# Both copies of the context mask are loaded into the wide block's idle space during the last self attention, and turned behind the last ranks

## The chip, the cores and the metric

The kernel runs on one core of one Trainium2 chip. The metric is the device time of one execution in microseconds (us), as the median of several runs. The kernel before takes 3855.7 us (three runs, 3854.54 to 3859.91).

An engine's name in a view: PE is TensorE (matmul), PEld its weight load, DVE is VectorE, ACT is ScalarE, POOL is GpSimd, SP is SyncE, whose queue (SPq) starts most of the DMAs. "L1530" is line 1530 of the kernel before.

## The reference

A batch of 4 sequences of 512 tokens (width 256) goes through two layers; each has an attention to a context of 1601 rows and then a block on the tokens alone. Gates (`tanh`) scale what is added to `x`. Cut to its steps:

```python
x = x + tanh(g_xattn[0]) * cross_attention_0(layernorm(x), ctx)        # 16 heads of 64, softmax over 1601
y = layernorm(x)                                                       # gated block 0
y = rmsnorm(y + grouped_query_self_attention(y))                       # 16 heads of 16, 4 of keys and values
y = rmsnorm(y + experts(y))                                            # sigmoid gate, top 2 of 8, capacity 640
x = x + tanh(g_ffn[0]) * y
e = where(mask == 0, -1e20, einsum(q = layernorm(x), k = ctx))         # masked cross attention, 16 heads of 16
x = x + tanh(g_xattn[1]) * (softmax(e / 16) @ ctx @ w_out.T + b_out)   # mask: int32, 512 x 1601
x = x + tanh(g_ffn[1]) * (self_attention(layernorm(x)) + dense_top2_experts(layernorm(x)))
```

The mask is one array for all sequences and heads. The masked attention needs it twice: with queries on the partitions (maskQ, 4 tiles of 128 x 1601) to take the row maxima, and with keys on the partitions (maskT, 12 tiles of 124 x 512 and one of 113 x 512) to add it to the scores.

## The kernel before

The work has four stages: the wide cross attention (block 1) with the self attention of gated block 0 (block 2) woven into it batch by batch; the experts; the masked cross attention (block 3); and block 4 woven into that. The work is a list of units, such as `("turn_e", e, f)`. `build_order` makes the list by a small model of the engines, and every engine then runs through the same list and emits its own part of each unit in that order. So the list is also the order of each queue: SP starts the DMAs of the list one after another, and a DMA whose condition isn't met yet holds up all DMAs behind it.

Most of the memory is two areas per partition, `wide` and `slim`, that the stages use anew. In the wide attention `wide` holds its context, keys, values and exponentials; in the experts stage the same area holds expert weights (`w1_sb`, `w2_sb` from 0), `rows_out` (4096), `rows_in` (6656), `rows_inT` (9216) and `hidden` (11776). `slim` holds block 2's data, and from the experts stage on what block 3 needs: both masks in bf16 (`maskT_sb` at 0, `maskQ_sb` at 3328), keys, values.

At the place of the change (after the last batch of block 2):

- `ranks 3` (DVE) makes the slot numbers of the last batch's tokens; `scatter 3` is 8 indirect DMAs (L1411), whose descriptors POOL makes, that put the token rows into `padded_x` in DRAM.
- `load_rows e` (SP, L961) brings the 640 rows of expert e; experts 0 and 1 first, expert e+2 once `turn_e e` has run on PE. `turn_e` (L1241) transposes them, `up` (L1249) and `down` (L1268) are the two products of an expert. `load_up` (L965) and `load_down` (L968) bring its weights, two experts ahead, `store_rows` (L971) writes its result.
- `mask_keys_in` loads maskT as int32 into `slim` from 6656 on, in two DMAs (L975, L976); DVE turns it into bf16 with -1e20 where the mask is 0 (`mask_keys`, L1530 and L1532). `mask_rows_in` (L978) loads maskQ into the same place and so waits until DVE has turned the first; then DVE turns that (`mask_rows`, L1536).
- Behind these, `load_k` and `load_v` (L981, L985, L986) load context keys and values of the first two groups of block 3, and POOL casts the keys (L1466).

`unit_of_last_down`, `wide_done` (the last PE unit that reads the wide attention's data) and `slim_done` (block 2's last `gate2`) are the marks on which units of later stages wait.

Of the kernel before, what the change touches and what calls it, by code (L numbers as in the profile page):

```python
# [7 lines left out]
B, S, D = 4, 512, 256  # L8
CTX = 1601
# [8 lines left out]
QT = S // P  # L18
FT = D // P
LN_EPS, RMS_EPS = 1e-5, 1e-6  # L20
MASKED = -1e20
# [4 lines left out]
CTX_TILE = 124  # L26
# [9 lines left out]
TOKENS = CAPACITY // P  # L36
HALF = CAPACITY // 2


# [181 lines left out]
def weave(streams, pace, slack):  # L221
# [10 lines left out]
    "setup": (0, 1, 2, 11),  # L232
    "mask_keys": (0, 0, 2, 0), "mask_rows": (0, 0, 1, 0),
    "ln": (0, 1, 14, 0), "turn": (1, 1, 0, 0),
# [26 lines left out]
def landing(unit):  # L261
    k = unit[0]
    if k in ("load_pair", "load_wo", "load_we", "load_up", "load_down", "load_rows", "store_rows"):
        return f"{k}{unit[-1] % 2}", 1
    if k in ("load_k", "load_v"):
        return f"{k}{unit[2] % 2}", {"load_k": 1, "load_v": 2}[k]
    if k in ("load_x", "gather"):
        return f"{k}{unit[1]}", {"load_x": 1, "gather": 2 * QT}[k]
    fixed = {"load_const": 3, "load_small": 10, "load_ctxT": 1, "mask_keys_in": 2, "mask_rows_in": 1, "load_gqa": 3,
             "clear": 3, "scatter": 2 * QT, "load_w4": 2, "store_x": 1}  # L270
    alike = {"mask_keys_in": "mask_in", "mask_rows_in": "mask_in"}
    return (alike.get(k, k), fixed[k]) if k in fixed else None

# [26 lines left out]
def build_order(plan):  # L300
# [21 lines left out]
    def on(unit, *marks):  # L322
        plan.tile_free[unit] = tuple(marks)
        return unit

    def emit(*units):
        order.extend(units)
        return units[-1]
# [199 lines left out]
    def experts_fill(wide_done):  # L528
        hidden_free, xT_free = [wide_done] * 2, [wide_done] * 2
        out_free = [wide_done] * 2  # L530
# [42 lines left out]
    def masks_fill(slim_done):  # L573
        emit(on(("mask_keys_in",), *slim_done))
        yield Step(use=(("ve", 4.0),), name=("mask_keys",), late=15.0)
        unit = emit(("mask_keys",))
        emit(on(("mask_rows_in",), ("vector", unit)))
        yield Step(use=(("ve", 4.0),), needs=(unit,), name=("mask_rows",))
        unit = emit(("mask_rows",))
        for s in range(2):  # L580
            k3_free[s] = v3_free[s] = (("vector", unit),)
        free["b3"] = slim_done
        free["xnT3"] = slim_done
        for g in range(2):
            load_keys(0, g)
        yield Step(use=(("po", 4.0),), needs=(unit,), name=("cast_k", 0, 0), late=6.0)
        emit(on(("cast_k", 0, 0), *free["b3"]))
# [54 lines left out]
    def four_experts(b):  # L642
# [7 lines left out]
        for e in range(EXPERTS):  # L650
# [11 lines left out]
           Stream(each_batch(two_made), 21.9, MADE_2), Stream(each_batch(two_used), 43.4, USED_2)], pace, SLACK_1)  # L662
    emit(*(on((f"load_{n}", e), *wide_done) for e in range(2) for n in ("up", "down")))
    slim_done = (("tensor", ("gate2", B - 1)),)
    emit(*(on(("load_rows", e), *wide_done) for e in range(2)))
    weave([Stream(experts_fill(wide_done), 156.0), Stream(masks_fill(slim_done), 1.0)], pace, SLACK_1)
# [27 lines left out]
def flamingo(nc, t, out):  # L694
    plan = Plan()
    order, bank_of, slot_of = plan.order, plan.bank, plan.slot
    ctx = ExitStack()
    with ctx:
# [110 lines left out]
        maskQ_sb = half(slim, 3328, QT, CTX)  # L809
        mask_keys_i = slim[:, 6656:6656 + NKT * S].bitcast(I32).rearrange("p (k n) -> p k n", k=NKT)  # L810
        mask_rows_i = slim[:, 6656:6656 + QT * CTX].bitcast(I32).rearrange("p (q n) -> p q n", q=QT)
        kq_3 = part(slim, 6656, 2 * (CTX + S))
# [99 lines left out]
        def _(sp):  # L912
            past = Past(sp)
            for unit in order:
# [58 lines left out]
                elif kind == "mask_keys_in":  # L973
                    body, rest_rows = key_rows(t["maskT"])
                    sp.dma_start(mask_keys_i[0:CTX_TILE, 0:full, :], body).then_inc(done_sem, 16)  # L975
                    sp.dma_start(mask_keys_i[0:tail_rows, full, :], rest_rows).then_inc(done_sem, 16)  # L976
                elif kind == "mask_rows_in":
# [23 lines left out]
        def _(pe):  # L1001
            past = Past(pe)
            past.wait_ge(*at("vector", "setup"))
            for unit in order:
# [166 lines left out]
                elif kind == "scoreb":  # L1171
# [7 lines left out]
                    if blk == 3:  # L1179
                        past.wait_ge(*at("vector", "mask_rows"))  # L1180
                        for h in range(2):
                            pe.matmul(head_bank(unit, h), ident_b[0:kn, :], maskT_sb[0:kn, k, :],  # L1182
                                      start=True, stop=False)
# [286 lines left out]
        def _(ve):  # L1470
# [45 lines left out]
            for unit in order:  # L1516
# [11 lines left out]
                elif kind == "mask_keys":  # L1528
                    past.wait_ge(*at("dma", "mask_keys_in"))
                    ve.tensor_scalar(maskT_sb[0:CTX_TILE, 0:full, :], mask_keys_i[0:CTX_TILE, 0:full, :], 0.0, MASKED,  # L1530
                                     ALU.is_equal, ALU.mult).then_inc(vector_done, 1)
                    ve.tensor_scalar(maskT_sb[0:tail_rows, full, :], mask_keys_i[0:tail_rows, full, :], 0.0, MASKED,  # L1532
                                     ALU.is_equal, ALU.mult).then_inc(vector_done, 1)
                elif kind == "mask_rows":
                    past.wait_ge(*at("dma", "mask_rows_in"))
                    ve.tensor_scalar(maskQ_sb, mask_rows_i, 0.0, MASKED, ALU.is_equal, ALU.mult).then_inc(vector_done, 1)  # L1536
                elif kind == "ln":
# [322 lines left out]
```

## Time and profile before

| | |
|---|---|
| median of 3 runs | 3855.7 us (3854.54 to 3859.91) |
| the profiled execution: its own time, its span | 3866.64 us, 3864.7 us |
| PE busy | 3496.2 us (90%), 18248 matmuls |
| DVE busy | 1989.6 us (51%) |
| ACT busy | 1435.3 us (37%) |
| POOL busy | 997.1 us (26%) |
| DMA | 108.28 MB, mean 28 GB/s |
| mean granted clock of TensorE | 0.925 of full speed |
| chain that ended last | PE 84%, DVE 7%, ACT 4%, another core or an unknown queue 2%, POOL 2% |

The time is that of the slowest (here the only) core. The span is what the profile covers of the profiled execution; 1.94 us of its own time lie around it. All times in the rows are us from the start of the span. The profile cuts the span into 40 slices of 96.6 us; PE is busy in nearly all of them at 9 tenths or more, and less in the 20th to the 25th, in which the last self attention, the experts and the start of block 3 lie.

### The profile page before, as it was taken

To read this page: it belongs to the slowest core of one execution; us is meant where nothing else is said; L and a number is where in the kernel's file an instruction comes from. 1 tells how busy PE (TensorE), PEld (TensorE's weight loads), DVE (VectorE), ACT (ScalarE), POOL (GpSimd) and SP (SyncE) were. 2 spreads that over 40 slices of the span, in tenths; PEclk is the share of its full clock that TensorE was granted. 3 is DMA by queue.
4 is the path that set the end of the run, shared out by engine and by line. 5 is a ranking of instruction groups with operands and counts; after the bars stand their busy time and mean duration, and the time that the engine had idled before them with its cause. 6 is when DMAs were issued, how large, how long until landed. Compare 5 with 4: busy or idle time off the path is not lost.

```text
span 3864.7 us, 44052 instructions
## 1 busy us (share of the span) xinstructions
PE 3496.2 (90%) x18248; PEld 1472.8 (38%) x18248; DVE 1989.6 (51%) x3277; ACT 1435.3 (37%) x1639; POOL 997.1 (26%) x481
## 2 busy tenths in 40 slices
PE   7999999989999899998754938989999999999987
PEld 3444443434434344343223812234323422342252
DVE  3445455454654545554330065655665566556444
ACT  3334344333444344443221203342454244334513
POOL 3556445454454554445200030000000000000000
PEclk9999999989999899998767958999999999899987
DMA  3000000000000100000004311010100100010000
GB/s 143 12 12 28 12 12 6 12 34 12 12 6 12 36 10 12 6 8 13 22 12 139 123 57 42 18 35 19 37 20 23 34 23 18 23 34 23 1 17 6
DMA packets 65934, 108.28 MB, mean 28 GB/s; under 512 B 4589, under 2 KB 49285, under 8 KB 65222
## 3 DMA queue, kind: packets, MB, share of 16 engines
q1 hardware_dynamic: 62662, 97.08, 7.9%
q0 software_dynamic: 3072, 8.39, 0.7%
q8 instruction: 143, 2.34, 0.2%
q14 instruction: 57, 0.47, 0.0%
HBM read 88.68 MB, written 16.78 MB: 27 GB/s over the span
## 4 chain that ended last, share of the span: by engine, by line
PE 84%; DVE 7%; ACT 4%; another core or an unknown queue 2%; POOL 2%; issue 1%; DMA 0%; DVEq 0%; ACTq 0%; SPq 0%; POOLq 0%
PE ring L1189 12%; PE pv L1082 10%; PE ring L1071 9%; PE pv L1210 8%; PE ring L1150 4%; PE ring L1052 3%; PE ring L1182 3%; PE ring L1195 3%; PE ring L1068 3%; PE ring L1029 2%; PE ring L1043 2%; PE ring L1044 2%; PE ring L1030 2%; PE ring L1268 2%; PE ring L1097 2%
## 5 line engine op out<-in xcount | busy, mean ns | idle before, releaser
L1452 POOL TENSOR_TENSOR wide<-wide 124x1024 f32<-124x1024 f32 (+1 forms) x352 | 827.9, 2352 | 268.5 <-ACT wide L1351 254.8
L1358 ACT ACTIVATE wide<-ring 124x1024 f32<-124x1024 f32 (+2 forms) x544 | 530.4, 1023 | 641.0 <-PE ring L1189 636.6
L1587 DVE CUSTOM_DVE_ANT_0 slim<-ring,slim 128x802 bf16<-128x802 f32 x512 | 508.3, 993 | 273.0 <-PE ring L1150 239.7
L1351 ACT ACTIVATE wide<-ring 124x1024 f32<-124x1024 f32 (+1 forms) x416 | 425.9, 1025 | 582.7 <-PE ring L1071 547.2
L1571 DVE TENSOR_REDUCE max_a<-ring 128x2 f32<-128x802 f32 x512 | 507.8, 994 | 242.9 <-PE ring L1052 242.4
L1082 PE MATMUL pv<-wide 124*64 124x512 f32 (+1 forms) x1664 | 453.2, 624 | 25.6 <-ACT wide L1351 25.6
L1071 PE MATMUL ring<-wide 64*124 64x512 f32 (+1 forms) x1664 | 429.0, 594 | 0.0
L1189 PE MATMUL ring<-slim 32*128 32x512 f32 x2176 | 405.2, 676 | 11.7 <-DVE slim L1612 7.5
L1597 DVE TENSOR_REDUCE slim<-ring 128x2 f32<-128x1024 f32 x256 | 309.2, 1222 | 192.6 <-PE ring L1162 189.5
L1466 POOL CAST slim<-slim 128x1601 bf16<-128x1601 f32 x16 | 24.4, 1523 | 1315.2 <-DMA slim<-in_ctx_k 965.3
L1150 PE MATMUL ring<-slim 32*128 32x401 bf16 x1024 | 233.2, 360 | 45.8 <-DVE max_b L1587 33.4
L1449 POOL TENSOR_TENSOR wide<-wide 124x1024 f32<-124x1024 f32 x32 | 75.3, 2353 | 637.2 <-PE pv L1082 451.8
L1210 PE MATMUL pv<-wide,slim 124*32 124x512 f32 (+1 forms) x1664 | 223.5, 609 | 1.7 <-ACT wide L1358 1.7
L1189 PEld LDWEIGHTS ring<-slim 32*128 32x128 f32 x2176 | 135.9, 193 | 172.7 <-issue 100.0
L1082 PEld LDWEIGHTS pv<-wide 124*64 124x64 f32 (+1 forms) x1664 | 83.5, 136 | 265.4 <-issue 214.4
L1052 PE MATMUL ring<-wide 64*128 64x401 bf16 x1024 | 175.8, 340 | 7.1 <-DVE max_a L1571 5.8
L1068 PE MATMUL ring<-wide,select_b 64*128 64x512 bf16 x832 | 160.8, 383 | 14.2 <-ACT wide L1351 12.2
L1150 PEld LDWEIGHTS ring<-slim 32*128 32x128 bf16 x1024 | 56.1, 95 | 293.6 <-ACT wide L1358 132.8
L1071 PEld LDWEIGHTS ring<-wide 64*124 64x124 f32 (+1 forms) x1664 | 157.3, 185 | 22.5 <-issue 2.9
L1561 DVE CAST wide<-wide 128x800 bf16<-128x800 f32 x64 | 37.1, 579 | 244.4 <-ACT wide L1328 174.7
L1043 PE MATMUL ring<-wide 128*124 128x128 f32 (+1 forms) x832 | 160.0, 274 | 0.0
L1044 PE MATMUL ring<-wide 128*124 128x128 f32 (+1 forms) x832 | 159.4, 272 | 0.0
(233 smaller groups left out, 4084.0 us busy)
## 6 DMA issues: line engine op xcount, KB each, us to landing
slim<-in_ctx_k SPq DMA_DIRECT2D x16, 800.5 KB, 4.4
wide<-in_w_pair SPq DMA_DIRECT2D x32, 384.0 KB, 3.1
slim<-in_ctx_v SPq DMA_DIRECT2D x16, 744.0 KB
wide<-in_w SPq DMA_DIRECT2D x16, 512.0 KB, 5.2
wide<-in_we SPq DMA_DIRECT2D x16, 512.0 KB, 3.6
wide<-in_ctxT SPq DMA_DIRECT2D x4, 1601.0 KB, 7.4
wide<-padded_x SPq DMA_DIRECT2D x8, 640.0 KB, 7.3
expert_rows<-wide SPq DMA_DIRECT2D x8, 640.0 KB, 3.8
```

What stands on the lines that cost most here:

```text
L1052: last = pe.matmul(slot[:, h * BANK:h * BANK + CHUNK], queries_ab[own, q * P:(q + 1) * P], keys_ab[own, c0:c0 + CHUNK], start=True, stop=True)
L1071: last = pe.matmul(slot[0:kn, h * BANK:(h + 1) * BANK], keys_a[own, p % 2, k0:k0 + kn], queries_a[own, p % 2, :], start=False, stop=True)
L1082: last = pe.matmul(pv_a[64 * h:64 * h + 64, :], values_a[0:kn, p % 2, k, 64 * h:64 * h + 64], exps_a[0:kn, slot_of["scorea", b, p, k], h * ...
L1150: last = pe.matmul(slot[:, j * BANK:j * BANK + CHUNK], queries_low(3, g)[own, q * P:(q + 1) * P], keys_low(3)[own, c0:c0 + CHUNK], start=T ...
L1189: last = pe.matmul(head_bank(unit, h), key_columns(blk, g, k0)[own, :], queries_place(blk, g)[own, :], start=blk != 3 or h >= 2, stop=blk ...
L1210: last = pe.matmul(pv_of[blk][PAD * h:PAD * h + PAD, :], value_columns(blk, g, k, kn, h), exps_tile(blk, b, g, k, h)[0:kn, :], start=k == ...
L1351: sc.activation(exps_a[0:kn, slot_of[unit], :], slot[0:kn, :], ACT.Exp, scale=WIDE ** -0.5).then_inc(scalar_done, 1)
L1358: sc.activation((exps_2 if blk == 2 else exps_34)[0:kn, first + 2 * i:first + 2 * i + 2, :].rearrange("p h n -> p (h n)"), ring_t[0:kn, ba ...
L1452: po.tensor_tensor(sums[0:kn, :], sums[0:kn, :], view, ALU.add).then_inc(pool_done, 1)
L1571: ve.reduce_max(max_a[:, :, q, c], slot.rearrange("p (h n) -> p h n", h=2)[:, :, 0:CHUNK], AX.X).then_inc(vector_done, 1)
L1587: ve.tensor_tensor_reduce(out=max_junk.rearrange("p (j n) -> p j n", j=2), in0=two[:, :, 0:CHUNK], in1=maskQ_sb[:, q, c0:c0 + 2 * CHUNK].r ...
L1597: ve.tensor_reduce(neg_cols[blk][:, q, 2 * hp * PAD:2 * hp * PAD + PAD + 1:PAD], slot.rearrange("p (h n) -> p h n", h=2), AX.X, ALU.max, n ...
```

## The change

The list is changed around the experts' start, and with it where the int32 masks lie.

- The int32 masks no longer go to `slim` but into parts of `wide` that the wide attention has left: maskQ where `rows_inT` and `hidden` come to lie (from 9216), nine tiles of maskT from 15872, the other four (three full, one of 113 rows) where `rows_out` comes to lie (from 4096). The two no longer share a place.
- Both loads are emitted behind the first experts' weights and wait for `wide_done` alone. maskT is loaded in three DMAs instead of two.
- DVE turns both right behind `ranks 3` and waits for `slim_done`, since the bf16 masks overwrite block 2's data; it does so in four instructions instead of three, and each mask has its own semaphore.
- The first evacuations of `turn_e` wait for `mask_rows`, those of `up` for `mask_keys` (ACT).
- `load_k`, `load_v` and `cast_k` of the first groups wait for `slim_done` only, but are emitted later in the list: behind `turn_e 3`, before the second half of `down 1`, where they stood behind `turn_e 2` before.

```diff
 COUNTS = {
-    "mask_keys": (0, 0, 2, 0), "mask_rows": (0, 0, 1, 0),
+    "mask_keys": (0, 0, 3, 0), "mask_rows": (0, 0, 1, 0),
...
     def experts_fill(wide_done):
-        hidden_free, xT_free = [wide_done] * 2, [wide_done] * 2
+        hidden_free, xT_free = [(("vector", ("mask_keys",)),)] * 2, [(("vector", ("mask_rows",)),)] * 2
...
     def masks_fill(slim_done):
-        emit(on(("mask_keys_in",), *slim_done))
-        yield Step(use=(("ve", 4.0),), name=("mask_keys",), late=15.0)
-        unit = emit(("mask_keys",))
-        emit(on(("mask_rows_in",), ("vector", unit)))
-        yield Step(use=(("ve", 4.0),), needs=(unit,), name=("mask_rows",))
-        unit = emit(("mask_rows",))
+        yield Step(needs=(("turn_e", 3, 1),))
         for s in range(2):
-            k3_free[s] = v3_free[s] = (("vector", unit),)
+            k3_free[s] = v3_free[s] = slim_done
...
-        yield Step(use=(("po", 4.0),), needs=(unit,), name=("cast_k", 0, 0), late=6.0)
+        yield Step(use=(("po", 4.0),), name=("cast_k", 0, 0), late=6.0)
...
     emit(*(on((f"load_{n}", e), *wide_done) for e in range(2) for n in ("up", "down")))
+    emit(on(("mask_rows_in",), *wide_done), on(("mask_keys_in",), *wide_done))
     slim_done = (("tensor", ("gate2", B - 1)),)
+    emit(on(("mask_rows",), *slim_done), on(("mask_keys",), *slim_done))
     emit(*(on(("load_rows", e), *wide_done) for e in range(2)))
...
-        mask_keys_i = slim[:, 6656:6656 + NKT * S].bitcast(I32).rearrange("p (k n) -> p k n", k=NKT)
-        mask_rows_i = slim[:, 6656:6656 + QT * CTX].bitcast(I32).rearrange("p (q n) -> p q n", q=QT)
+        mask_keys_i = wide[:, 15872:15872 + STAGED * S].bitcast(I32).rearrange("p (k n) -> p k n", k=STAGED)
+        mask_rest_i = wide[:, 4096:4096 + (NKT - STAGED) * S].bitcast(I32).rearrange("p (k n) -> p k n", k=NKT - STAGED)
+        mask_rows_i = wide[:, 9216:9216 + QT * CTX].bitcast(I32).rearrange("p (q n) -> p q n", q=QT)
...
-                    sp.dma_start(mask_keys_i[0:CTX_TILE, 0:full, :], body).then_inc(done_sem, 16)
-                    sp.dma_start(mask_keys_i[0:tail_rows, full, :], rest_rows).then_inc(done_sem, 16)
+                    sp.dma_start(mask_keys_i[0:CTX_TILE, :, :], body[:, 0:STAGED, :]).then_inc(done_sem, 16)
+                    sp.dma_start(mask_rest_i[0:CTX_TILE, 0:full - STAGED, :], body[:, STAGED:full, :]).then_inc(done_sem, 16)
+                    sp.dma_start(mask_rest_i[0:tail_rows, full - STAGED, :], rest_rows).then_inc(done_sem, 16)
```

In SP's queue, from the first experts' weights (`w1`, `w2` of experts 0 and 1) to the second stored result, `in_maskT` and `in_maskQ` are the masks, `padded_x` the experts' rows, `in_ctx_k` and `in_ctx_v` keys and values of block 3. Before:

```order
84 L965 DMA wide<-in_w1 128x1024
85 L968 DMA wide<-in_w2 128x1024
86 L961 DMA wide<-padded_x 128x5x256 x2
87 L975 DMA slim<-in_maskT 124x12x512
88 L976 DMA slim<-in_maskT 113x512
89 L978 DMA slim<-in_maskQ 128x4x1601
90 L961 DMA wide<-padded_x 128x5x256 x2
91 L965 DMA wide<-in_w1 128x1024 x2
92 L961 DMA wide<-padded_x 128x5x256
93 L981 DMA slim<-in_ctx_k 128x1601
94 L985 DMA slim<-in_ctx_v 124x12x128
95 L986 DMA slim<-in_ctx_v 113x128
```

And the same stretch now (the lines of the new kernel are one to two lower here):

```order
85 L966 DMA wide<-in_w2 128x1024
86 L977 DMA wide<-in_maskQ 128x4x1601
87 L973 DMA wide<-in_maskT 124x9x512
88 L974 DMA wide<-in_maskT 124x3x512
89 L975 DMA wide<-in_maskT 113x512
90 L959 DMA wide<-padded_x 128x5x256 x4
91 L963 DMA wide<-in_w1 128x1024 x2
92 L959 DMA wide<-padded_x 128x5x256
93 L969 DMA expert_rows<-wide 128x5x256
94 L966 DMA wide<-in_w2 128x1024
95 L963 DMA wide<-in_w1 128x1024
96 L959 DMA wide<-padded_x 128x5x256
```

The masks stand ahead of the first two experts' rows, the rows of experts 2 and 3 directly behind those, and the keys and values (from row 97 on) one expert later.

On DVE, at the end of `ranks 3` (the last two small operations) and the start of the experts' results. Before:

```order
798 L1800 TENSOR_TENSOR prob<-combine,pick 128x32
799 L1802 TENSOR_REDUCE shares<-prob 128x4 [waits vector_done]
800 L1530 TENSOR_SCALAR slim<-slim 124x6144 [waits landed_mask_in]
801 L1532 TENSOR_SCALAR slim<-slim 113x512
802 L1536 TENSOR_SCALAR slim<-slim 128x6404 [waits landed_mask_in]
803 L1809 COPY wide<-ring 128x768 [waits tensor_done]
```

Now:

```order
799 L1807 TENSOR_REDUCE shares<-prob 128x4 [waits vector_done]
800 L1541 TENSOR_SCALAR slim<-wide 128x6404 [waits landed_mask_rows_in]
801 L1531 TENSOR_SCALAR slim<-wide 124x4608 [waits landed_mask_keys_in]
802 L1533 TENSOR_SCALAR slim<-wide 124x1536
803 L1535 TENSOR_SCALAR slim<-wide 113x512
804 L1814 COPY wide<-ring 128x768 [waits tensor_done]
```

The turns keep their place in DVE's order, but the rows' mask now comes first and the keys' mask takes three instructions. They wait for loads that stand further ahead in SP's queue, past the ones for the experts' rows.

## Rows read from the trace of the kernel before

**Rows 1.** Page, the span in 40 slices: granted clock of TensorE in tenths

```profile
PEclk9999999989999899998767958999999999899987
```

**Rows 2.** Windows: stretch, busy by engine (instructions), clock, DMA share, GB/s

```profile
2054.40:2100.80 46.40, 0.00 (x0) 0.00 (x0) 5.63 (x3) 0.70 (x1) 0.00 (x0) 0.54 0.40 132
2100.80:2113.00 12.20, 12.17 (x51) 10.78 (x52) 2.51 (x2) 1.41 (x2) 1.52 (x1) 0.80 0.75 258
2113.00:2230.00 117.00, 117.00 (x520) 94.25 (x519) 11.55 (x14) 24.12 (x35) 0.00 (x0) 1.00 0.38 120
```

**Rows 3.** Timeline of PE: start, us, line, operation, tile, count, [idle before <-releaser]

```profile
2036.50 17.89 PE L1249 MATMUL ring<-wide 128*128 128x320 f32 x64
2100.83 2.37 PE L1241 MATMUL ring<-consts,wide 128*128 128x128 f32 x10 [46.45 <-DMA wide<-padded_x]
2102.99 10.12 PE L1268 MATMUL ring<-wide 128*128 128x256 f32 x40
...
2121.57 1.25 PE L1241 MATMUL ring<-consts,wide 128*128 128x128 f32 x10
2122.66 8.80 PE L1268 MATMUL ring<-wide 128*128 128x256 f32 x40
...
2141.13 8.87 PE L1268 MATMUL ring<-wide 128*128 128x256 f32 x40
...
2177.89 8.80 PE L1268 MATMUL ring<-wide 128*128 128x256 f32 x40
```

**Rows 4.** Timeline of SP's queue, DMA issues from 1867 to 2135 us

```profile
1867.48 0.43 SPq L968 DMA_DIRECT2D wide<-in_w  x1
2027.60 0.95 SPq L961 DMA_DIRECT2D wide<-padded_x  x2
2028.59 0.47 SPq L975 DMA_DIRECT2D slim<-in_maskT  x1
...
2088.47 0.40 SPq L978 DMA_DIRECT2D slim<-in_maskQ  x1
2088.91 1.07 SPq L961 DMA_DIRECT2D wide<-padded_x  x2
...
2103.23 0.38 SPq L961 DMA_DIRECT2D wide<-padded_x  x1
...
2134.91 1.26 SPq L968 DMA_DIRECT2D wide<-in_w  x1
```

**Rows 5.** Timeline of DVE, the turns of the masks

```profile
2084.74 3.36 DVE L1530 TENSOR_SCALAR slim<-slim 124x6144 bf16<-124x6144 int32 x1 [68.78 <-DMA slim<-in_maskT]
2088.02 0.42 DVE L1532 TENSOR_SCALAR slim<-slim 113x512 bf16<-113x512 int32 x1
...
2098.86 3.50 DVE L1536 TENSOR_SCALAR slim<-slim 128x6404 bf16<-128x6404 int32 x1 [10.42 <-DMA slim<-in_maskQ]
```

**Rows 6.** Timeline of POOL, first and last of the last scatter's eight

```profile
2016.25 0.98 POOL L1411 DMA_INDIRECT padded_x<-src,places  x1 [158.58 <-DVE shares L1802]
...
2025.17 0.97 POOL L1411 DMA_INDIRECT padded_x<-src,places  x1 [0.30 <-issue]
```

**Rows 7.** Timeline around 825 us, a POOL addition and DVE beside it

```profile
822.38 4.86 POOL L1452 TENSOR_TENSOR wide<-wide 124x1024 f32<-124x1024 f32 x2 [0.18 <-ACT wide L1351]
...
825.33 1.95 DVE L1780 TENSOR_TENSOR prob<-prob,hit 128x32 f32<-128x32 f32 x1
...
827.42 0.19 DVE L1785 TENSOR_TENSOR prob<-prob,pick 128x32 f32<-128x32 f32 x1
```

**Rows 8.** Timeline around 2247 us, indirect DMAs of POOL and DVE beside them

```profile
2247.09 0.95 POOL L1421 DMA_INDIRECT wide<-expert_rows,sources  x1 [0.30 <-issue]
2248.34 1.07 POOL L1421 DMA_INDIRECT wide<-expert_rows,sources  x1 [0.30 <-issue]
...
2247.32 3.38 DVE L1729 SCALAR_TENSOR_TENSOR src<-wide,shares,src 128x256 f32<-128x256 f32 x8 [15.69 <-DMA wide<-expert_rows,sources]
```

**Rows 9.** Windows: the stretch from block 3 in full swing to the end

```profile
2440.00:3865.00 1425.00, 1336.12 (x7109) 501.18 (x7108) 808.70 (x1519) 559.83 (x610) 20.76 (x14) 0.93 0.08 22
```

More of the change, by code:

```diff
@@ L37 @@
 HALF = CAPACITY // 2
+STAGED = 9
 HOP = 0.2
@@ L268, in landing @@
         return f"{k}{unit[1]}", {"load_x": 1, "gather": 2 * QT}[k]
-    fixed = {"load_const": 3, "load_small": 10, "load_ctxT": 1, "mask_keys_in": 2, "mask_rows_in": 1, "load_gqa": 3,
+    fixed = {"load_const": 3, "load_small": 10, "load_ctxT": 1, "mask_keys_in": 3, "mask_rows_in": 1, "load_gqa": 3,
              "clear": 3, "scatter": 2 * QT, "load_w4": 2, "store_x": 1}
-    alike = {"mask_keys_in": "mask_in", "mask_rows_in": "mask_in"}
-    return (alike.get(k, k), fixed[k]) if k in fixed else None
+    return (k, fixed[k]) if k in fixed else None
 class Plan:
@@ L1179, in _ @@
                     if blk == 3:
-                        past.wait_ge(*at("vector", "mask_rows"))
+                        past.wait_ge(*at("vector", "mask_keys"))
                         for h in range(2):
@@ L1529, in _ @@
                     past.wait_ge(*at("dma", "mask_keys_in"))
-                    ve.tensor_scalar(maskT_sb[0:CTX_TILE, 0:full, :], mask_keys_i[0:CTX_TILE, 0:full, :], 0.0, MASKED,
+                    for lane, other in plan.tile_free[unit]:
+                        past.wait_ge(*at(lane, *other))
+                    ve.tensor_scalar(maskT_sb[0:CTX_TILE, 0:STAGED, :], mask_keys_i[0:CTX_TILE, :, :], 0.0, MASKED,
                                      ALU.is_equal, ALU.mult).then_inc(vector_done, 1)
-                    ve.tensor_scalar(maskT_sb[0:tail_rows, full, :], mask_keys_i[0:tail_rows, full, :], 0.0, MASKED,
+                    ve.tensor_scalar(maskT_sb[0:CTX_TILE, STAGED:full, :], mask_rest_i[0:CTX_TILE, 0:full - STAGED, :], 0.0, MASKED,
+                                     ALU.is_equal, ALU.mult).then_inc(vector_done, 1)
+                    ve.tensor_scalar(maskT_sb[0:tail_rows, full, :], mask_rest_i[0:tail_rows, full - STAGED, :], 0.0, MASKED,
                                      ALU.is_equal, ALU.mult).then_inc(vector_done, 1)
@@ L1535, in _ @@
                     past.wait_ge(*at("dma", "mask_rows_in"))
+                    for lane, other in plan.tile_free[unit]:
+                        past.wait_ge(*at(lane, *other))
                     ve.tensor_scalar(maskQ_sb, mask_rows_i, 0.0, MASKED, ALU.is_equal, ALU.mult).then_inc(vector_done, 1)
```

## The prediction

> **What bounds the kernel now.** I read the page's chain first: PE has 84% of it, so an edit counts only where PE stands still or waits to restart. The slices say where: the granted clock of TensorE falls to 5 to 7 tenths in the middle and is 9 almost everywhere else [rows 1]. The windows there are clear-cut. From 2054.4 to 2100.8 us PE does nothing at all, the clock is 0.54 and the DMA engines are busy 40%; the next 12.2 us run at 0.80, and then 117 us at 1.00 with PE busy all of the time [rows 2]. So one hole of 46.4 us lies in the experts stage, and behind it PE is the bound.
>
> The timeline of PE names the hole's end: the transposes of expert 2 waited 46.45 us for its rows (`padded_x`) [rows 3]. SP's queue tells why they were late. The rows of experts 0 and 1 went out at 2027.60, maskT at 2028.59, and then SP stood at maskQ until 2088.47, because maskQ was to go where the int32 maskT still lay; the rows of experts 2 and 3 stood behind it and went out at 2088.91 [rows 4]. DVE could turn maskT only at 2084.74, after 68.78 us of idling for it [rows 5]. The load of maskT takes 2084.74 - 2028.59 = 56.15 us; maskQ, slightly larger, took 2098.86 - 2088.47 = 10.4 us [rows 4, 5]. The chain is thus: scatter, slow maskT load, turn, SP released, rows land, PE. The idle time is no lack of bandwidth, but the order of a queue.
>
> **The change part by part.**
>
> *The hole.* SP no longer waits for DVE. The rows of experts 2 and 3 go out when PE has transposed those of experts 0 and 1, before the 64 `up` matmuls that begin at 2036.50 and end at 2054.39 [rows 3]. A pair of such loads took from 2088.91 until the wait ended at 2100.83, 11.9 us [rows 3, 4]; begun at 2036.5 they land by 2048.4, 6 us before PE wants them. So all of the 46.45 us goes.
>
> *The restart.* After the hole PE ran at a low clock (0.80 over 12.2 us [rows 2]). Ten transposes took 2.37 us where the next expert's took 1.25, and forty `down` matmuls 10.12 where the next took 8.80 [rows 3]: 1.12 + 1.32 = 2.44 us. Without the hole PE goes from one matmul to the next, so this goes too. Together **-48.9 us**.
>
> *The loads of the masks.* They now follow the first experts' weights, at about 1868 [rows 4], and need 10.4 + 56.15 = 66.6 us one behind the other, if the three DMAs of maskT move as the two did. They land by about 1935, 81 us before the last ranks end at 2016 (POOL starts on them at 2016.25 [rows 6]). Block 2 takes all its data from on chip in that time and SP issues nothing between 1868 and 2027 [rows 4], so nothing is behind them: 0 us. If that cover were gone, each us beyond 2016 would show in the first evacuations of the experts, on ACT.
>
> *The turns.* DVE works 3.50 + 3.36 + 0.42 = 7.28 us as before, some 0.1 more for the fourth instruction. It starts at 2016.0, where it idled [rows 5], and is done at 2023.3; behind it in DVE's queue are only the first experts' results. The evacuations that now wait for it come after the rows have landed, later than 2032. On DVE that is 0. But POOL makes the descriptors of the last scatter from 2016.25 to 2026.14, eight times [rows 6], and the whole chain to PE waits for that scatter. In the trace before, DVE idles through all of it. What does 7.3 us of DVE work beside it cost? The lower end is almost nothing: beside eight DVE operations of 0.42 us each, one of POOL's indirect DMAs took 1.07 us against 0.95 [rows 8]. The upper end is that they exclude each other: a tiny DVE operation took 1.95 us instead of 0.19 while POOL's addition ran, and ended with it at 827.28 [rows 7]. Then the first indirect DMA starts at 2023.3 instead of 2016.25: 7.0 us. I take **+7.0**. The turns are single instructions of up to 3.5 us, back to back, reading and writing SBUF only; they leave no gaps as the short ones of [rows 8] do, and the one place where the trace shows the two engines in each other's way shows a wait to the other's very end.
>
> The Trainium skill has a rule for exactly this ("SBUF — State Buffer", "Who interferes with whom"): a DVE cast or tensor_scalar in a two-port mode and GpSimd hold the same port pair as an exclusive lock, and whoever comes second stands still; the section before it adds that GpSimd then cannot write descriptors. By that rule the cost is the 7.0; it also says that operations with two SBUF inputs probably don't hold up descriptors, and with that the 0.12 us of [rows 8] agrees. No row here has such a DVE operation beside a scatter.
>
> *Keys and values.* SP issues the four large loads of block 3's keys and values right behind an expert's rows. Before, that was behind the rows of expert 4; from their issue at 2103.23 to that of the next weights for `down` (expert 2) at 2134.91 SP needed 31.7 us, mostly on them [rows 4]. `down 2` began at 2141.13, 37.9 us after 2103.23, and 18.47 after `down 1` (2122.66), where two experts together take 2177.89 - 2141.13 = 36.76, or 18.38 each [rows 3]. So the weights were just in time, at the most 0.1 us late. Now the loads go out one expert later, behind the rows of expert 5, and `down 3` must have its weights. From those rows' issue to `down 3` are two experts less the 0.2 us between `down`'s start and the issue, 36.5 us. The margin shrinks by 1.4 us, since the slow restart is no longer in it. The cost lies between 0 (the queue is emptier than at 2103) and 1.5; I take **+1.0**. The result of expert 1 is stored later, but its place is written again only by `down 3`'s evacuation.
>
> *Sum.* -48.9 + 7.0 + 1.0 = -40.9 us. In the profiled execution: 3866.64 - 40.9 = 3825.7. The median of the runs was 3855.7, 10.9 lower than this execution, so the forecast for the median is 3855.7 - 40.9 = **3814.8 us**, 1.1% less.
>
> **The rivals.**
>
> *The scatter is not held up.* For it: rows 8, 0.12 us. Then the turns are free, the sum is -47.9, and the time 3807.8. Against it: these are long instructions without gaps.
>
> *The keys and values starve `down 3` and what follows.* SP needs 31.7 us for them whatever PE does, and the margin is spent. If the weights of `down 3` and then those of `up 5` each come some 5 us late (the loads wait behind the values' small packets), the sum is -48.9 + 7 + 10 = -31.9, 3823.8. Against it: before, the second set behind the block was no problem, since PE ran without a gap from 2113 to 2230 [rows 2].
>
> *The change doesn't do what it says.* If the masks landed after the ranks, ACT would hold the experts instead. maskT would have to take over 81 us longer than its 56. Each us beyond that costs one; at 20 us late the time is 3834.8. Against it: nothing else uses the DMA engines there.
>
> *Slower: the hole was a rest that paid for clock.* From 2440 on PE is busy 1336.12 of 1425 us at a mean clock of 0.93 [rows 9]. If PE without its pause were granted less there, its busy time would grow. Since 40.9 us are gained, the time is that of before when 1336.12 x (0.93 / c - 1) = 40.9, at a mean clock of c = 0.902; at 0.89 it costs 60.1 us, and the time is 3874.9. Against it: PE has run 117 us without a gap at 1.00 [rows 2], and the low clocks there stand in and behind its idle time.
>
> **How the numbers follow.** The forecast has 0.58 (delayed scatter, small loss on the weights), the free scatter 0.27, starved weights 0.09, late masks 0.03, the slower case 0.03. The medians of two sets of runs differ by about 3 us by chance (the three of before span 5.4). For 8 times in 10 the range takes the free scatter with that error, 3807.8 - 3.3, and goes up to the starved case: 3804.5 to 3823.5. A change of this kernel's time is told from none at about 0.2%, 7.7 us. All cases but the slower one and half of the late masks are far beyond that: faster 0.95, same 0.02, slower 0.03.
>
> **What would show it.** In the new profile the window behind the first 64 `up` matmuls has PE busy throughout, and the transposes of expert 2 take 1.25 us. DVE's turns lie at 2016 to 2023.3 and do not wait for a DMA. The first of POOL's last eight scatters shows right or wrong the 7.0: it lasts some 8 us, or starts late, or is 1 us as before, and PE's first expert transposes begin at 2039 instead of 2032.17. At `down 3` PE waits 0 to 1.5 us for `in_w`. The forecast is wrong if PE waits for the masks through ACT, if a new gap of more than a few us stands at `down 3` or `up 5`, or if the mean clock from the experts on falls below 0.93.

## The result and the profile after

| | before | after |
|---|---|---|
| median | 3855.1 us (4 runs, 3846.6 to 3859.9) | 3816.6 us (4 runs, 3813.3 to 3820.2) |
| profiled execution: own time, span | 3866.64, 3864.7 us | 3817.63, 3815.6 us |
| mean granted clock | 0.925 | 0.932 |

The ratio is 0.9893 with a 95% interval of 0.9868 to 0.9918: 1.1% faster, 32 to 51 us. 3814.8 us was forecast.

The windows around the experts, in the order of the columns of [rows 2]:

```profile
2035.60:2057.40 21.80, 21.79 (x86) 16.18 (x87) 0.00 (x0) 9.03 (x12) 0.00 (x0) 0.91 0.30 100
2057.40:2112.00 54.60, 54.60 (x246) 43.88 (x245) 4.95 (x6) 12.02 (x18) 1.52 (x1) 1.00 0.49 149
2112.00:2185.00 73.00, 72.92 (x328) 59.37 (x326) 7.56 (x9) 14.01 (x20) 0.00 (x0) 1.00 0.34 112
```

PE is busy from the first transposes to the last `down`, and the clock goes up to 1.00 and stays there. Nothing is left of the hole of [rows 2]. PE's timeline answers [rows 3] (L1240 is the transposes, L1248 `up`, L1267 `down`; before they were L1241, L1249, L1268):

```profile
2035.58 4.30 PE L1240 MATMUL ring<-consts,wide 128*128 128x128 f32 x20 [25.66 <-DMA wide<-padded_x]
2039.88 17.49 PE L1248 MATMUL ring<-wide 128*128 128x320 f32 x64
2057.21 1.26 PE L1240 MATMUL ring<-consts,wide 128*128 128x128 f32 x10
2058.30 8.80 PE L1267 MATMUL ring<-wide 128*128 128x256 f32 x40
...
2112.23 1.25 PE L1240 MATMUL ring<-consts,wide 128*128 128x128 f32 x10
2113.57 8.87 PE L1267 MATMUL ring<-wide 128*128 128x256 f32 x40
...
2167.57 17.43 PE L1267 MATMUL ring<-wide 128*128 128x256 f32 x80
```

The transposes of expert 2 follow the first `up` with no wait and take 1.26 us instead of 2.37, the first `down` 8.80 instead of 10.12. At `down 3` (2113.57) there are 1.34 us from the transposes' start instead of the usual 1.09. In SP's queue (as [rows 4]; L977 maskQ, L973 to L975 maskT, L959 the experts' rows, L966 weights for `down`) the masks went out at 1866.6 and the rows of four experts in one go:

```profile
1866.61 0.46 SPq L977 DMA_DIRECT2D wide<-in_maskQ  x1
1867.11 0.46 SPq L973 DMA_DIRECT2D wide<-in_maskT  x1
1867.61 31.15 SPq L974 DMA_DIRECT2D wide<-in_maskT  x1
1898.80 11.44 SPq L975 DMA_DIRECT2D wide<-in_maskT  x1
2031.03 9.23 SPq L959 DMA_DIRECT2D wide<-padded_x  x4
...
2107.42 1.32 SPq L966 DMA_DIRECT2D wide<-in_w  x1
```

And DVE and POOL at the end of the ranks, both engines of one timeline in order of time (answers to [rows 5] and [rows 6]):

```profile
2014.16 0.19 DVE L1807 TENSOR_REDUCE shares<-prob 128x4 f32<-128x32 f32 x1
2014.27 3.49 DVE L1541 TENSOR_SCALAR slim<-wide 128x6404 bf16<-128x6404 int32 x1
2014.63 5.71 POOL L1410 DMA_INDIRECT padded_x<-src,places  x1 [158.31 <-DVE shares L1807]
2017.67 2.55 DVE L1531 TENSOR_SCALAR slim<-wide 124x4608 bf16<-124x4608 int32 x1
2020.13 0.96 DVE L1533 TENSOR_SCALAR slim<-wide 124x1536 bf16<-124x1536 int32 x1
2020.64 1.29 POOL L1410 DMA_INDIRECT padded_x<-src,places  x1 [0.30 <-issue]
2021.02 0.41 DVE L1535 TENSOR_SCALAR slim<-wide 113x512 bf16<-113x512 int32 x1
2022.23 0.97 POOL L1410 DMA_INDIRECT padded_x<-src,places  x1 [0.30 <-issue]
...
2028.61 0.97 POOL L1410 DMA_INDIRECT padded_x<-src,places  x1 [0.30 <-issue]
```

DVE no longer waits for a DMA. But the first indirect DMA of the scatter takes 5.71 us where it took 0.98, the second 1.29; from the third on they are as before. The eight start over 13.98 us instead of 8.92: the scatter is 5.06 us late.

**Where the time went.** One stretch can be compared without the luck of the clock elsewhere: from the end of the ranks (end of DVE's last small reduction) to the end of the last `down`. Before: 2015.97 to 2230.90, 214.93 us. After: 2014.35 to 2185.00, 170.65 us. The difference of -44.28 us has four pieces. From the ranks' end to the first transposes: 16.20 before, 21.23 after, +5.03. To the end of the first 64 `up` matmuls: 22.22 and 21.79, -0.43. From there to `down 0`: 48.60 and 0.93, -47.67. The rest: 127.91 and 126.70, -1.21, namely the slow restart of `down` gone (-1.32), `down 3` later (+0.31), and a delay of `down 2` gone. The spans differ by 49.1; the other 4.8 us lie ahead of the stretch (1.6) and behind it (3.2), where the work is unchanged. The medians differ by 38.5. The stretch differed by 1.4 us between two executions of the changed kernel (170.65 and 172.01, below); a median of this kernel is known to several us.

### The profile page after: what moved, and what is told of

It reads as the page before. It is cut to its first block and busy times, and to the rows that moved or that the text cites. A ratio compares the mean times of both kernels' runs of the same rounds, so it can differ in the third digit from the quotient of the medians.

```text
span 3815.6 us, 44056 instructions
## 1 busy us (share of the span) xinstructions
PE 3487.2 (91%) x18248; PEld 1464.8 (38%) x18248; DVE 1989.9 (52%) x3278; ACT 1435.6 (38%) x1639; POOL 1002.5 (26%) x481
## 5 line engine op out<-in xcount | busy, mean ns | idle before, releaser
L1592 DVE CUSTOM_DVE_ANT_0 slim<-ring,slim 128x802 bf16<-128x802 f32 x512 | 508.6, 993 | 273.7 <-PE ring L1149 240.9
L1188 PE MATMUL ring<-slim 32*128 32x512 f32 x2176 | 403.9, 674 | 11.7 <-DVE slim L1617 7.5
L1067 PE MATMUL ring<-wide,select_b 64*128 64x512 bf16 x832 | 160.8, 383 | 14.2 <-ACT wide L1350 12.2
```

The costliest lines, as they stand in the source:

```text
L1188: last = pe.matmul(head_bank(unit, h), key_columns(blk, g, k0)[own, :], queries_place(blk, g)[own, :], start=blk != 3 or h >= 2, stop=blk ...
L1592: ve.tensor_tensor_reduce(out=max_junk.rearrange("p (j n) -> p j n", j=2), in0=two[:, :, 0:CHUNK], in1=maskQ_sb[:, q, c0:c0 + 2 * CHUNK].r ...
```

## The experiments

The kernels ran on three chips, each beside executions of before on the same chip: the change once more, the turns behind the scatter (alone and with the values split) and the split of maskT beside 11 of before (median 3864.9 us); the last two rows beside 7 (3861.0); the three marked "once" ran once each beside one of before (3848.3), so their ratio has no interval. The stretch is the one above. "Wait" is PE's wait with a releaser between the first `up` and the last `down`.

| kernel | first indirect DMA | ranks' end to first transposes | PE's wait | stretch | ratio to before (95%) |
|---|---|---|---|---|---|
| before | 0.98 | 16.20 | 46.45 | 214.93 | 1 |
| after | 5.71 | 21.23 | none listed | 170.65 | 0.9893 (0.9868 to 0.9918) |
| the change once more | 5.71 | 21.23 | 1.44 | 172.01 | 0.9904 (0.9885 to 0.9922) |
| turns behind the scatter | 0.98 | 16.13 | 2.31 | 170.05 | 0.9856 (0.9833 to 0.9879) |
| the same, a reduction beside it | 0.99 | 16.15 | 1.59 | 167.74 | 0.9873, once |
| one turn beside it | 3.98 | 19.13 | 2.85 | 173.65 | 0.9927, once |
| short turns beside it | 1.13 | 16.71 | 2.49 | 168.91 | 0.9881, once |
| before, maskT split | 0.99 | 16.17 | 11.08 | 178.59 | 0.9910 (0.9892 to 0.9929) |
| turns behind, values split | 0.98 | 16.20 | none | 165.92 | 0.9856 (0.9832 to 0.9879) |
| that once more | 0.98 | 16.17 | none | 165.74 | 0.9889 (0.9868 to 0.9909) |
| another order, masks in slim, loads split | 0.99 | 16.16 | none | 165.72 | 0.9865 (0.9845 to 0.9884) |

### The change once more

> The changed kernel once more, unedited, beside the others on the same chip. Expected 1.0 to 1.2% below the kernel before, near 3815 us; the first of the last eight indirect DMAs takes 5.7 us again, the PE stretch from the first expert transposes to the end of the last down takes 149.4 us.

Measured: 3827.9 us beside a before of 3864.9, 1.0% less (before on this chip was 10 us slower than beside the first runs, so the 3815 us expected were not met, but the ratio was). The 5.71 us are as expected. From the first transposes to the last `down`'s end it took 2176.81 - 2026.03 = 150.8 us instead of 149.4; the 1.4 us more are a wait at `down 3` (below).

### What holds up the scatter: the turns moved

```diff
 elif kind == "mask_rows":
     past.wait_ge(*at("dma", "mask_rows_in"))
+    past.wait_ge(*at("dma", "scatter", B - 1))
```

> The changed kernel, with one more wait: DVE turns the masks only when the last scatter has landed. My theory (DVE's turns shut POOL out while it makes the scatter's descriptors): the first of POOL's last eight indirect DMAs takes 0.98 us instead of the 5.71 of the changed kernel, PE's first expert transposes start 16.2 us after the ranks end instead of 21.2, and the turns (7.4 us) lie beside the load of the experts' rows and the first up matmuls, where at most the first evacuation waits for the rows' turn (0 to 2 us). Time 3 to 5 us below the changed kernel, about 3812. Rival (the scatter was slow for another reason: more DMA traffic, or descriptor memory): the first indirect DMA still takes over 5 us and the time is that of the changed kernel, or 2 us more from the later turns.

The first indirect DMA is back at 0.98 us and the first transposes start 16.13 us behind the ranks: the turns had held it up. The theory's 3 to 5 us did not all reach the stretch (170.05 against 170.65 and 172.01). The first transposes and `up` took 22.44 us instead of 21.79, and `down 3` gave most of the rest back:

```profile
2096.41 1.26 PE L1240 MATMUL ring<-consts,wide 128*128 128x128 f32 x10
2099.97 10.49 PE L1267 MATMUL ring<-wide 128*128 128x256 f32 x40 [2.31 <-DMA wide<-in_w]
```

A wait of 2.31 us and a slow restart of 1.69 (10.49 against 8.80). The median, 3808.7, is 19 us below that of the change once more on the same chip, far more than the 2 us of the stretch. The two profiled executions differ by 2.0 us (3811.7 and 3809.7), both at a mean granted clock of 0.936; the other four of the change took 3826 to 3832 us at 0.930 or 0.931. So the rest goes with the clock, and nothing ties it to this edit: two sets of runs of one kernel (values split, and that once more) differ by 0.0033 in their ratio, some 13 us. That this edit frees the scatter is shown by the timeline, not by the time.

### Is it DVE being busy, or the kind of its operation?

Against the kernel with the turns behind the scatter:

```diff
     past.wait_ge(*at("dma", "mask_rows_in"))
+    ve.reduce_max(max_b[:, 0, 0, 0:1], wide[:, 9216:9216 + 6404], AX.X).then_inc(vector_done, 1)
     past.wait_ge(*at("dma", "scatter", B - 1))
```

> The kernel that turns the masks after the last scatter, with one extra DVE operation beside the scatter: a maximum over 6404 values per partition in SBUF (about 6.7 us), whose result nobody uses. Theory (what shuts POOL out is the kind of the turns, which move two values per cycle, not DVE being busy): the first indirect DMA takes about 1 us although DVE is busy as long as with the turns. Rival (any long DVE operation on SBUF holds POOL up, or DVE's bandwidth does): it takes 5 us or more.

DVE and POOL in the timeline:

```profile
2005.92 6.81 DVE L1539 TENSOR_REDUCE max_b<-wide 128x1 f32<-128x6404 f32 x1
2006.29 0.99 POOL L1410 DMA_INDIRECT padded_x<-src,places  x1 [149.68 <-DVE shares L1809]
2007.58 0.97 POOL L1410 DMA_INDIRECT padded_x<-src,places  x1 [0.30 <-issue]
```

DVE reads SBUF for 6.81 us in one instruction, and POOL takes 0.99 us where it took 0.98. So it is not DVE being busy that holds POOL up, but the kind of operation. The reduction takes 6.81 us for 6404 values, the turn 3.49 for as many: the turn moves values about twice as fast. The section that the prediction quoted from the Trainium skill ("SBUF — State Buffer", "Who interferes with whom") names `tensor_scalar` in a two-port mode as an operation that shuts GpSimd out and `tensor_reduce` as one that on this chip never does. The trace agrees with both (5.71 and 0.99 us).

The reduction also writes one value per partition where the turn writes 6404, and this run doesn't separate that from the rate. Rows of the changed kernel at the start of block 3 speak against the writing: from 2221.57 to 2230.02 POOL's indirect DMAs took 0.94 to 0.95 us each beside DVE operations (L1592) that write 802 values per partition to SBUF in 0.99 us. A slow writing operation as long as a turn was not run.

### How long POOL waits

One turn alone beside the scatter:

```diff
 elif kind == "mask_keys":
     past.wait_ge(*at("dma", "mask_keys_in"))
+    past.wait_ge(*at("dma", "scatter", B - 1))
```

> The changed kernel, but only the rows' mask (3.5 us, one instruction) is turned beside the last scatter; the keys' mask waits until the scatter has landed. Theory A (POOL waits for the DVE instruction that runs, and would have gone between the first two if it had been asked to): the first indirect DMA takes 0.98 + 3.1 = about 4.1 us at the most, and the scatter ends 2.5 to 3.5 us late instead of 5.06. Theory B (POOL was only held from the second turn on): the scatter is 1 us late or less.

```profile
2006.20 3.49 DVE L1542 TENSOR_SCALAR slim<-wide 128x6404 bf16<-128x6404 int32 x1
2006.57 3.98 POOL L1410 DMA_INDIRECT padded_x<-src,places  x1 [149.67 <-DVE shares L1808]
2010.85 0.97 POOL L1410 DMA_INDIRECT padded_x<-src,places  x1 [0.30 <-issue]
```

Theory A: 3.98 us, 3.00 late. POOL's instruction ends at 2010.55, 0.86 us behind the turn's end at 2009.69, which is nearly its whole undisturbed length. With all four turns (the changed kernel) it ends at 2020.34, only 0.12 behind the end of the second turn (2020.22). Both would fit if POOL needed what DVE holds twice, early in the instruction and again at its end: it got the first at the boundary between the turns (2017.7), worked, and was shut out again by the second turn until 2020.2. The traces show the ends; the two accesses are a guess from them that no run tested.

The same turns in 29 short instructions:

```diff
-    ve.tensor_scalar(maskQ_sb, mask_rows_i, 0.0, MASKED, ALU.is_equal, ALU.mult)
+    for q in range(QT):
+        for c0, c1 in ((0, 400), (400, 800), (800, 1200), (1200, CTX)):
+            ve.tensor_scalar(maskQ_sb[:, q, c0:c1], mask_rows_i[:, q, c0:c1], 0.0, MASKED, ALU.is_equal, ALU.mult)
...
-    ve.tensor_scalar(maskT_sb[0:CTX_TILE, 0:STAGED, :], mask_keys_i[0:CTX_TILE, :, :], 0.0, MASKED, ALU.is_equal, ALU.mult)
...
+    for k in range(NKT):
+        kn = CTX_TILES[k][1]
+        source = mask_keys_i[0:kn, k, :] if k < STAGED else mask_rest_i[0:kn, k - STAGED, :]
+        ve.tensor_scalar(maskT_sb[0:kn, k, :], source, 0.0, MASKED, ALU.is_equal, ALU.mult)
```

> The changed kernel with the same turns in short instructions: 16 of about 400 values for the rows' mask and 13 of 512 for the keys' mask, back to back beside the last scatter, 29 instead of 4. Theory A (POOL gets in at an instruction's end): each indirect DMA takes at most 0.4 us longer, the scatter ends 1 to 2 us late. Theory B (the lock is passed from one DVE instruction to the next while they follow without a gap): the first indirect DMA lasts until the turns are nearly done, 6 to 9 us, since the short instructions take some 10 us in all.

```profile
2005.93 5.05 DVE L1542 TENSOR_SCALAR slim<-wide 128x400 bf16<-128x400 int32 x16
2006.30 1.13 POOL L1410 DMA_INDIRECT padded_x<-src,places  x1 [151.26 <-DVE slim L1542]
...
2010.91 4.78 DVE L1534 TENSOR_SCALAR slim<-wide 124x512 bf16<-124x512 int32 x13
2011.57 1.09 POOL L1410 DMA_INDIRECT padded_x<-src,places  x1 [0.30 <-issue]
```

Theory A, and cheaper than it said: each indirect DMA takes 0 to 0.16 us longer, the eight start over 9.46 us instead of 8.92, 0.5 us late. DVE's work grows from 7.4 to 9.8 us, which nothing waits for. Instructions of 0.3 to 0.4 us back to back don't keep POOL out; one of 3.49 us does. Three of the eight took 1.09 us, 0.12 more than alone, which is also what [rows 8] show (1.07 against 0.95).

### How much of the hole is the load's length?

Against the kernel before:

```diff
-sp.dma_start(mask_keys_i[0:CTX_TILE, 0:full, :], body).then_inc(done_sem, 16)
-sp.dma_start(mask_keys_i[0:tail_rows, full, :], rest_rows).then_inc(done_sem, 16)
+for p0, p1 in ((0, 112), (112, CTX_TILE)):
+    sp.dma_start(mask_keys_i[p0:p1, 0:full, :], body[p0:p1]).then_inc(done_sem, 16)
+for p0, p1 in ((0, 112), (112, tail_rows)):
+    sp.dma_start(mask_keys_i[p0:p1, full, :], rest_rows[p0:p1]).then_inc(done_sem, 16)
```

> The kernel before, with one edit: maskT is loaded in four DMAs that split its partitions 112 + 12 (and the last tile's 113 as 112 + 1). Masks stay in slim, SP still waits for DVE, the turns stay where they were. Theory (the hole was the 56 us of the maskT load, which used 0.26 of the DMA engines because 124 partitions are spread badly): maskT lands in 10 to 15 us, at about 2042; SP sends maskQ at 2046 and the rows of experts 2 and 3 behind it, which land at about 2058; PE's hole shrinks from 46.45 to 2 to 6 us and the slow restart behind it mostly goes. Time about 3855 - 45 = 3810, as good as the change or a little better, since no turn stands beside the scatter. Rival (the load's rate is set by something else, such as its 2 KB pieces): the load still takes over 40 us and the time stays within 10 us of before.

Measured: 3829.4 us beside 3864.9, and the hole 11.08 us. In SP's queue L976 and L978 are the parts of maskT, L980 is maskQ, L961 the rows; then DVE's turns and PE:

```profile
2015.72 3.34 SPq L976 DMA_DIRECT2D slim<-in_maskT  x2
2019.10 1.55 SPq L978 DMA_DIRECT2D slim<-in_maskT  x2
2040.11 0.39 SPq L980 DMA_DIRECT2D slim<-in_maskQ  x1
2040.55 1.08 SPq L961 DMA_DIRECT2D wide<-padded_x  x2
```

```profile
2036.38 3.36 DVE L1532 TENSOR_SCALAR slim<-slim 124x6144 bf16<-124x6144 int32 x1 [33.28 <-DMA slim<-in_maskT]
...
2052.77 2.37 PE L1243 MATMUL ring<-consts,wide 128*128 128x128 f32 x10 [11.08 <-DMA wide<-padded_x]
2054.93 9.14 PE L1270 MATMUL ring<-wide 128*128 128x256 f32 x40
```

maskT now takes 20.7 us instead of 56.15. So the rival's 40 us is excluded: nine tenths of the load (2688 of 2976 KB) is still one DMA with the same pieces, only over 112 partitions instead of 124, and the DMA share of the windows during it is 0.80 to 1.06 instead of 0.24 (2054 to 2084 us of before). But I expected 10 to 15 us, and 2 to 6 for the hole. The load's last 8 us ran at 142 GB/s after some 280, and the hole was underestimated: from their issue, maskQ and the rows behind it need another 12.2 us. Splitting the load gives back 35 of the 46 us; the wait of SP's queue stays.

### How much of it is the order of the queue?

From the kernel before, with its masks in `slim`, split as above, and the values' loads too:

```diff
 def masks_fill(slim_done):
+    yield Step(needs=(("turn_e", 1, 1),))
     emit(on(("mask_keys_in",), *slim_done))
-    yield Step(use=(("ve", 4.0),), name=("mask_keys",), late=15.0)
+    yield Step(use=(("ve", 4.0),), needs=(("turn_e", 3, 1),), name=("mask_keys",))
     unit = emit(("mask_keys",))
     emit(on(("mask_rows_in",), ("vector", unit)))
-    yield Step(use=(("ve", 4.0),), needs=(unit,), name=("mask_rows",))
+    yield Step(use=(("ve", 4.0),), needs=(unit, ("turn_e", 4, 1)), name=("mask_rows",))
```

> The kernel before with the masks left in slim and only their loads and turns placed elsewhere in the list: maskT's load (split 112 + 12 as in the kernel with the split load) behind the rows of experts 2 and 3, its turn and maskQ's load behind the transposes of expert 3, maskQ's turn and the keys' and values' loads behind those of expert 4; value loads split as well. No load stands in idle space of wide. Theory (what the change gains is that the experts' rows no longer stand behind a wait for DVE in SP's queue; the early load and the other place are not needed for it): PE has no hole, and from the end of the ranks to the end of the last down it takes 166 us, as in the kernel with both cures (165.9), against 214.9 of before. Time 1.4% below before. Rival (the masks' traffic in the experts stage takes from the experts' loads): PE waits for rows or weights, 3 to 15 us in total.

```profile
2026.39 9.43 SPq L962 DMA_DIRECT2D wide<-padded_x  x4
2035.86 1.48 SPq L977 DMA_DIRECT2D slim<-in_maskT  x2
...
2082.39 0.38 SPq L981 DMA_DIRECT2D slim<-in_maskQ  x1
```

No hole, no wait, 165.72 us, and 1.35% below before. maskQ still waits for the turn of maskT, but by then maskT has long landed. So loading early and the place in `wide` are not needed for what the change gains, once the loads are split; it is enough that the experts' rows no longer stand behind a wait in SP's queue. Moving the masks was one way to get that, and the way that put the turns beside the scatter. What the order gives without the splits is open. I expect that an unsplit maskT would hold SP in the midst of the experts, as it did before (34.40 us on L976), but the order without them was not run.

### `down 3` and the value loads

Against the kernel with the turns behind the scatter:

```diff
-sp.dma_start(v_3[0:CTX_TILE, g % 2, 0:full, :], body).then_inc(done_sem, 16)
-sp.dma_start(v_3[0:tail_rows, g % 2, full, :], rest_rows).then_inc(done_sem, 16)
+for p0, p1 in ((0, 112), (112, CTX_TILE)):
+    sp.dma_start(v_3[p0:p1, g % 2, 0:full, :], body[p0:p1]).then_inc(done_sem, 16)
+for p0, p1 in ((0, 112), (112, tail_rows)):
+    sp.dma_start(v_3[p0:p1, g % 2, full, :], rest_rows[p0:p1]).then_inc(done_sem, 16)
```

> As the kernel that turns the masks after the last scatter, and besides the values of block 3 are loaded with their partitions split 112 + 12 (last tile 112 + 1). Theory (the value loads hold SP for some 28 us because their 124 partitions use few DMA engines): the four key and value loads of the first two groups hold SP under 15 us instead of 27.4, and down 3 starts 1.09 us after its transposes as the others do, instead of 1.34. Later value loads are hidden, so the time is that of the other kernel less 0.3 us, which the time alone can't show. Rival: the rate of these loads is set by their 512 byte pieces; SP is held as long as before and down 3 still is 0.25 us late.

In SP's queue (L980 keys, L985 and L987 values, L969 the stored result):

```profile
2067.17 0.53 SPq L980 DMA_DIRECT2D slim<-in_ctx_k  x1
2067.74 4.16 SPq L985 DMA_DIRECT2D slim<-in_ctx_v  x2
2071.93 0.75 SPq L987 DMA_DIRECT2D slim<-in_ctx_v  x2
...
2078.88 0.39 SPq L969 DMA_DIRECT2D expert_rows<-wide  x1
```

They hold SP 11.7 us instead of the 27.4 of the changed kernel, and `down 3` follows its transposes by 1.10 us. The stretch is 165.92, all that the removed hole and its restart could give: 214.93 - 165.92 = 49.0, against the 48.9 worked out in the prediction. The 0.3 us of the first profile was the lucky case: without the split `down 3` waited 1.4 to 2.9 us in five other executions. In every one of them it started 6.15 to 6.17 us after SP had sent its weights (2107.42 to 2113.57 in the changed kernel, 2099.22 to 2105.38 once more, 6.22 in [rows 3, 4] of before). What varies is how long the keys' and values' loads held SP.

> The kernel with the turns behind the last scatter and the split value loads, once more and unedited, on the chip of the other. Expected: 1.3 to 1.5% below before, 166 us from the end of the ranks to the end of the last down. If the gain over the changed kernel was luck of the chip's clock, the stretch will still be 166 us but the time only 1.0% below.

The stretch again took 165.74 us, but the time was 3819.8 beside 3861.0, 1.1% below before and not 1.3 to 1.5, between the two outcomes that I had named. The stretch's gain over the change (5 to 6 us) is there each time; in the total it drowns.

## Why the prediction was right

*The hole* and *the restart* (-48.9): right, in place and size; the kernel without the two side costs shows 49.0. The cause was the wait of SP's queue and not bandwidth, as said; the kernel with the masks in `slim` and another order has no hole either, though the masks' bytes move beside the experts there (its loads were split as well). The length of maskT's load made up 35 us of the hole, since SP's wait lasted as long as that load.

*The masks' loads* (0) were hidden. *The turns* on DVE (0): hidden too.

*The scatter* (+7.0): the mechanism was right, the size was 5.06. The step that was mis-sized is "then the first indirect DMA starts at 2023.3". It took POOL to be shut out until the last turn's end. POOL's instruction ends with the second turn (5.71 us instead of 0.98), the next one takes 0.32 us longer beside the last two turns, and the other six run as before. The upper bound from [rows 7] was the right kind of row, an exclusion to the other instruction's end, but that is the end of one instruction and not of a row of them. The rival "the scatter is not held up" fell, with a chance of 0.27. What it went by, [rows 8], were short operations of 0.42 us; short turns cost as little (0 to 0.16 us), so these rows could not tell what long ones do.

*Keys and values* (+1.0, between 0 and 1.5): 0.31 in the profiled execution, 1.4 to 2.9 in others, with the slow restart behind the wait 4.0 (turns behind the scatter, 2.31 + 1.69) and 4.4 (one turn beside it, 2.85 + 1.53). The margin was read rightly as spent; I took the 31.7 us of SP as fixed, and it varies from 30.6 to 33.3 with a wait behind it that doesn't. The upper bound was too low.

*Sum*: -40.9 forecast; -44.3 in the stretch; -38.5 in the medians. In the profiled execution both side costs were smaller than forecast (by 2.0 and 0.7 us), and 0.6 us came from what the sum didn't have: the first `up` 0.43 faster, a delay of 0.20 at `down 2` gone. In the other executions with unsplit values the loss at `down 3` was larger than forecast, so there the two errors have opposite signs. That the median came within 2 us of the forecast is luck: the interval of the gain spans 19 us. The slower rival (clock) fell: behind 2390 us the mean clock over 1425 us is

```profile
2390.00:3815.00 1425.00, 1336.03 (x7126) 497.16 (x7124) 811.51 (x1521) 561.12 (x612) 20.76 (x14) 0.93 0.08 22
```

the 0.93 and the 1336 us of [rows 9].

**The better version.** The turns behind the scatter with split value loads (0.9856 and 0.9889), and the masks in `slim` with another order (0.9865), both have stretches of 165.7 to 165.9 us and beat the change by 5 us there. Against before each is clearly faster. Against the changed kernel the time is no clear witness: beside the change once more on the same chip the first of them is faster beyond both intervals (0.9832 to 0.9879 against 0.9885 to 0.9922), by more than its stretch explains, and the same kernel run again overlaps the change (0.9868 to 0.9909).

## What to carry to other kernels

Where an engine waits for a transfer, look at what stood ahead of it in the issuing queue: a single DMA that waits for a buffer delays every one behind it, and moving it past the urgent ones was worth as much here, with split loads, as giving it a buffer of its own. Long DVE operations like these turns don't belong beside GpSimd's indirect DMAs: they cost 5 us there, 0.5 us in short pieces, and behind the scatter nothing. And the loads over 124 partitions here were not only slow, they held their queue; 112 + 12 was a cheap cure.

## What the runs showed that I had not expected

- A DMA's issue can hold SP for tens of us when the loads ahead of it are slow: 31.15 and 11.44 us on two parts of maskT, 11 to 13.5 us on a values' tail of 56.5 KB.
- A short wait of PE sometimes costs more than itself. After 2.31 and 2.85 us `down` took 10.49 and 10.33 us, after 1.44, 1.59 and 2.49 us it took 8.87. The granted clock tells them apart. With the turns behind the scatter (first two rows) it is at its lower level, 0.50 or 1.2 GHz, right behind the wait, then 0.69, and back at 1.00 from 2104 on; with the short turns (last two rows) it stays at 1.00, or 2.4 GHz, through a longer wait. What decides whether it falls is open; the length of the wait alone does not:

```profile
2097.60:2100.00 2.40, 0.09 (x2) 0.06 (x1) 0.00 (x0) 0.90 (x2) 0.00 (x0) 0.97 0.98 302
2100.00:2102.00 2.00, 2.00 (x5) 1.64 (x6) 0.00 (x0) 0.00 (x0) 0.00 (x0) 0.50 0.88 241
2101.00:2103.50 2.50, 0.01 (x2) 0.04 (x1) 0.00 (x0) 0.84 (x2) 0.00 (x0) 1.00 0.96 302
2103.50:2105.50 2.00, 2.00 (x9) 1.78 (x10) 0.00 (x0) 0.00 (x0) 0.00 (x0) 1.00 0.86 244
```

- In six profiled executions (the change once more, turns behind the scatter, the split of maskT, the splits together in both of their runs, and the order in slim) DVE stood still twice (with the turns behind the scatter one such row is listed, of 3.95 us) at the start of block 3, for nothing that the profile names, and block 3's first row transposes came 82 to 83 us after its first `turn`. In the profiles of before and after and of the three kernels that ran once it was some 73 us. The rows are of the change once more:

```profile
2218.74 0.99 DVE L1592 CUSTOM_DVE_ANT_0 slim<-ring,slim 128x802 bf16<-128x802 f32 x1 [3.91 <-remote]
...
2224.33 0.99 DVE L1592 CUSTOM_DVE_ANT_0 slim<-ring,slim 128x802 bf16<-128x802 f32 x1 [4.59 <-remote]
```

The change once more had it and the change's first profile had not, so it belongs to no edit; its cause is open. Before's medians beside these six kernels were 3864.9 and 3861.0, against 3855.1 beside the change's first runs and 3848.3 beside the three that ran once; no profile of before was taken there, so that it has the stall too isn't shown. It is one reason why the stretch and not the span was compared.
